# Attention values of a head as one 129-column operand, its two halves summed on VectorE

## The chip, the cores and the metric

One core of a Trainium2 chip runs the whole program. The metric is the device time of one execution in microseconds (us); lower is better. TensorE (PE) multiplies matrices, and its weight loads are listed apart (PEld). VectorE (DVE), ScalarE (ACT) and GpSimd (POOL) work element by element. SP is the queue that issues the DMAs.

## The reference

The reference is one block of a gated cross-attention transformer: `x` is (2, 256, 128), the context (2, 512, 128). The attention part is what the change touches:

```python
q1, k1, v1 = split(x1 @ Wq1), split(x1 @ Wk1), split(x1 @ Wv1)   # 8 heads of 64
k2, v2 = split(x2 @ Wk2), split(x2 @ Wv2)
k, v = concat([k1, k2]), concat([v1, v2])                        # 768 keys
attn = softmax(einsum('bihd,bjhd->bhij', q1, k) * scale)
out = einsum('bhij,bjhd->bihd', attn, v).reshape(B, N1, h * d) @ Wo + bo
x = x + tanh(g_xattn) * out
```

Behind it stands a mixture of eight experts with one shared expert (two of eight by a top-k gate, hidden width 512, exact gelu), added with a second gate.

## The kernel before, in words

Single-precision products are made from half-precision ones: a value is held as a high f16 part and a low f16 part, and high x high, high x low and low x high are summed in PSUM. There are 2 batches x 8 heads = 16 heads; two heads of a batch make a pair, and a pair has three units of 2 x 128 keys. Each engine runs its own list of instructions, written out by one loop over steps; semaphores tie the lists together. Step s handles score unit s (24 units), and other work is set beside it:

- `scores(u)` (L1105) on PE, then the exponential (`exp_unit`, L646) and the high part of the probabilities (`make_hi`, L654) on ACT, then the low part, `p_lo` = `prob` - `p_hi`, on POOL (`prob_lo`, L554; both inputs lie in SBUF).
- `max_chunk(p, c)` on PE (L1088 for c = 0 and 1, L1093 for c = 2) and `part_max` on DVE (L821) find the row maxima of the pair two or three steps ahead. Each chunk's matmul waits until DVE has finished the chunk before it, because both use the same two PSUM banks.
- `shift_row` (L1103, PE) and `shift_out` (L837, DVE) turn the maxima of a pair into the shift of its scores.
- `item_of` projects keys, queries and values of the next pairs or batch on PE (L991 to L993); ACT takes the high part out of PSUM (L635), DVE the low part (L804), one step later.
- `values(j)` (L1149) on PE multiplies the probabilities of head j with its values: 2 query tiles x 6 key tiles, three matmuls each (L1170 to L1172): `p_hi` with the 65 columns of `v_hi` (64 values and a column of ones for the sum of the row), `p_hi` with the 64 columns of `v_lo`, `p_lo` with the 65 of `v_hi`. The probabilities are the 128x128 weights. All go into one place, `o_ps`, in PSUM bank 6.
- `reciprocals(j)` (L844) and `normalise(j)` (L849) on DVE wait for `values(j)`, invert the two row sums and multiply: `o_ps` times `rsum` (in SBUF, two numbers for each row, each broadcast over 64 columns) goes to `o_sb`. `normalise` raises `o_done`, for which the next `values` waits, because there is one `o_ps`.

From step 5 on the pattern has three steps. In a step with s mod 3 = 2 (5, 8, 11, ...) PE does scores, values of a pair's first head, the shift row, the maxima c = 0, an item; with s mod 3 = 0 scores, values of the second head, the maxima c = 1, an item; with s mod 3 = 1 scores, the maxima c = 2, an item, and no values. DVE's order in a step is: low part of the item of the step before, `shift_out`, `reciprocals`, `normalise`, `part_max`. The first six pairs have their values in steps 5 to 21; maxima end with step 19. Steps 23 to 26 hold the last four heads, beside the first matmuls of the experts, which fill the rest.

```python
            def reciprocals(j):
                dve.wait_ge(pv_ps, QT * (j + 1))
                mark(nc.vector.reciprocal(rsum[:, j, :], o_ps[:, :, DH]))
```

`mark` counts an instruction, and `settle` makes DVE wait until all that are counted have been written.

Of the kernel before, what the change touches and what calls it, by code (L numbers as in the profile page):

```python
# [13 lines left out]
F32 = mybir.dt.float32  # L14
F16 = mybir.dt.float16
ALU = mybir.AluOpType
# [3 lines left out]
P = 128  # L20
B = 2
# [3 lines left out]
HEADS = 8  # L25
DH = 64
INNER = HEADS * DH
PAIRS = HEADS // 2
KEYS = T1 + T2
KT = KEYS // P  # L30
QT = T1 // P
NT = B * QT
# [21 lines left out]
KT2 = 2  # L54
UPP = KT // KT2
NPAIR = B * PAIRS
# [35 lines left out]
def chunk_of(s):  # L92

    p, c = divmod(s - CHUNK0, UPP)
    return (p, c) if 0 <= p < NPAIR else None
# [62 lines left out]
def before(n, banks):  # L158

    return max([m + 1 for m in range(n) if banks_of(m) & set(banks)], default=0)  # L160


def items_ready(*items):

    return max(ITEMS.index(it) for it in items) + 1
# [55 lines left out]
def block_kernel(nc, x, ctx_in, g_xattn, g_ffn, Wq1, Wk1, Wv1, Wk2, Wv2, Wo, bo,  # L221
                 gate_w, gate_b, w1, b1, w2, b2, ws1, bs1, ws2, bs2, out):
    stack = ExitStack()
    with stack:
        def sb(name, shape, dt):
            return stack.enter_context(nc.sbuf_tensor(name, shape, dt))

        def sem(name):
            return stack.enter_context(nc.semaphore(name))
# [9 lines left out]
        wf = sb("wf", [P, 2, NE, 2, 512], F16)  # L239
        k_both = sb("k_both", [P, B, 2, PAIRS, KEYS], F16)  # L240
        k_nat = k_both[:, :, :, :, :].rearrange("p b a h n -> p a b h n")
# [12 lines left out]
        shift = sb("shift", [P, 2, T1], F16)  # L254
        part = sb("part", [P, 2, 2, 2, QT], F32)
        nmax = sb("nmax", [P, 2, P], F32)
        v_hi = sb("v_hi", [P, B * KT, HEADS, DH + 1], F16)
        v_lo = sb("v_lo", [P, B * KT, HEADS, DH], F16)
        p_hi = sb("p_hi", [P, RINGP, 2, KT2 * T1], F16)
        p_lo = sb("p_lo", [P, RINGP, 2, KT2 * T1], F16)  # L260
        o_sb = sb("o_sb", [P, NT, INNER], F32)
# [39 lines left out]
        banks = stack.enter_context(nc.psum_tensor("banks", [P, 8, 512], F32))  # L301

        def span(first, n):

            return banks[:, first:first + 2, :].rearrange("p a n -> p (a n)")[:, 0:n]
# [7 lines left out]
            first = 2 + 2 * score_buf(u)  # L313
            return banks[:, first:first + 2, :]

        o_ps = banks[:, 6, 0:QT * (DH + 1)].rearrange("p (q d) -> p q d", q=QT)
        shift_ps_rows = banks[:, 6, 512 - P:]
        misc = banks[:, 7, :]

# [33 lines left out]
        o_done = sem("o_done")  # L353
# [29 lines left out]
        def ring_f(j):  # L383

            return ring[:, (3 + j) % RING]
# [15 lines left out]
        def item_out(n):  # L401

            kind = ITEMS[n][0]
            return span(BANK[n], KEYS) if kind == "k" else banks[:, BANK[n], :]

# [189 lines left out]
        def _(act):  # L595
# [18 lines left out]
            def item_of(n):  # L614
# [16 lines left out]
                else:  # L631
                    _, b, t = item
                    dst, s = v_hi[:, b * KT + t, :, 0:DH], 1.0 / S_W
                    src = src.rearrange("p (h d) -> p h d", d=DH)
# [97 lines left out]
        def _(dve):  # L732
# [3 lines left out]
            def mark(ins):  # L736

                nonlocal n_chain
                n_chain += 1
                ins.then_inc(dve_chain, 1)  # L740

            def settle():

                dve.wait_ge(dve_chain, n_chain)
# [35 lines left out]
            def item_of(n):  # L780
# [19 lines left out]
                else:  # L800
                    t = item[1] * KT + item[2]
                    dst, hi, s = v_lo[:, t, :, :], v_hi[:, t, :, 0:DH], 1.0 / S_W
# [39 lines left out]
            def reciprocals(j):  # L842
                dve.wait_ge(pv_ps, QT * (j + 1))
                mark(nc.vector.reciprocal(rsum[:, j, :], o_ps[:, :, DH]))  # L844

            def normalise(j):
                b, h = divmod(j, HEADS)
                settle()
                nc.vector.tensor_tensor(o_sb[:, QT * b:QT * b + QT, h * DH:(h + 1) * DH], o_ps[:, :, 0:DH],  # L849
                                        rsum[:, j, :].unsqueeze(2).broadcast_to([P, QT, DH]),  # L850
                                        ALU.mult).then_inc(o_done, 1)

# [75 lines left out]
            for i in range(CHUNK0, STEPS):  # L928
# [18 lines left out]
                if values_of(i) is not None:  # L947
                    reciprocals(values_of(i))
                    normalise(values_of(i))
                if chunk_of(i) is not None:  # L950
                    p, c = chunk_of(i)
# [9 lines left out]
                if 0 <= k < NF:  # L961
                    b, e = k // NE, EORDER[k % NE]
# [25 lines left out]
        def _(pe):  # L988
            def three(dst, w, a, start=True, stop=True):

                nc.tensor.matmul(dst, w[0], a[0], start=start, stop=False)  # L991
                nc.tensor.matmul(dst, w[0], a[1], start=False, stop=False)  # L992
                return nc.tensor.matmul(dst, w[1], a[0], start=False, stop=stop)  # L993

            def w_pair(w, cols):
                return wa[:, 0, w, cols], wa[:, 1, w, cols]

            def x_pair(cols):
                return xT[:, 0, cols], xT[:, 1, cols]
# [13 lines left out]
            def read_out(n):  # L1013

                if n > 0:
                    pe.wait_ge(item_lo, n)

            def item_of(n):
# [15 lines left out]
                elif kind == "k":  # L1034
# [6 lines left out]
                    pe.wait_ge(item_lo, ITEMS.index(("tx", 0)) + 1)  # L1041
                    last = three(dst[:, T2:KEYS], w_pair(WK1, pair), x_pair(slice(b * T1, (b + 1) * T1)))
                elif kind == "q":
# [19 lines left out]
            def q_of(p, half, hl, cols):  # L1063

                b, pp = divmod(p, PAIRS)
                return q_nat[DH * half:DH * half + DH, hl, b, pp, cols]

            def k_of(p, half, hl, cols):

                b, pp = divmod(p, PAIRS)  # L1070
                return k_nat[DH * half:DH * half + DH, hl, b, pp, cols]

            def max_chunk(p, c):
# [16 lines left out]
                else:  # L1090
                    for q in range(QT):
                        for half in range(2):
                            last = nc.tensor.matmul(banks[:, half, q * T1:(q + 1) * T1],  # L1093
                                                    q_of(p, half, 0, slice(q * P, q * P + P)),
                                                    k_of(p, half, 0, slice(T2, KEYS)), start=True, stop=True)
                last.then_inc(max_ps, 1)
# [52 lines left out]
            def values(j):  # L1149

                p, half = divmod(j, 2)
                b, h = divmod(j, HEADS)
                if j == 0:
                    read_out(before(NI, [6]))
                else:
                    pe.wait_ge(o_done, j)
                if h == 0:
                    pe.wait_ge(item_lo, items_ready(*[("v", b, t) for t in range(KT)]))
                for q in range(QT):
                    for t in range(KT):  # L1160
                        u = UPP * p + t // KT2
                        if half == 0 and q == 0 and t % KT2 == 0:
                            if u == LO_LAST:
                                pe.wait_ge(pd_done, 1)
                            else:
                                pe.wait_ge(pl_done, u + 1)
                        cols = slice(t % KT2 * T1 + q * P, t % KT2 * T1 + q * P + P)
                        vh, vl = v_hi[:, b * KT + t, h, :], v_lo[:, b * KT + t, h, :]
                        ph, pl = p_hi[:, u % RINGP, half, cols], p_lo[:, u % RINGP, half, cols]
                        nc.tensor.matmul(o_ps[:, q, :], ph, vh, start=(t == 0), stop=False, skip_group_check=True)  # L1170
                        nc.tensor.matmul(o_ps[:, q, 0:DH], ph, vl, start=False, stop=False, skip_group_check=True)  # L1171
                        last = nc.tensor.matmul(o_ps[:, q, :], pl, vh, start=False, stop=(t == KT - 1),  # L1172
                                                skip_group_check=True)
                    last.then_inc(pv_ps, 1)

# [39 lines left out]
            for i in range(CHUNK0, STEPS):  # L1215
# [3 lines left out]
                if 0 <= k < NF:  # L1219
                    b, e = k // NE, EORDER[k % NE]  # L1220
# [17 lines left out]
                    for c in range(HC):  # L1238
                        cols = slice(c * P, (c + 1) * P)
                        dst = span(2 * (k % 2), HC * T1)[:, c * T1:(c + 1) * T1]  # L1240
                        if k in H32:
                            last = nc.tensor.matmul(dst, ring_f(k)[:, 0, cols], x2T[:, tok], start=True, stop=True)  # L1242
                        else:
                            last = three(dst, (wf[:, 0, e, 0, cols], wf[:, 1, e, 0, cols]),
                                         (x2h[:, 0, tok], x2h[:, 1, tok]))
                        if c % 2 == 1:
                            last.then_inc(h_ps, 1)
                if values_of(i) is not None:
                    values(values_of(i))
# [10 lines left out]
                if 0 <= k < NF:  # L1260
# [13 lines left out]
                    for q in range(QT):  # L1274
                        for c in range(HC):
                            at = c * T1 + q * P
                            cols = slice(c * P, (c + 1) * P)
                            if k in FULL32:
                                last = nc.tensor.matmul(banks[:, 4 + k % 2, q * D:(q + 1) * D],  # L1279
                                                        hid[:, k % NHID, at:at + P], ring_f(k % NE)[:, 1, cols],  # L1280
                                                        start=(c == 0), stop=(c == HC - 1))
                                continue
                            last = three(banks[:, 4 + k % 2, q * D:(q + 1) * D],
                                         (hid_hi[:, k % HB, at:at + P], hid_lo[:, k % HB, at:at + P]),
                                         (wf[:, 0, e, 1, cols], wf[:, 1, e, 1, cols]),
                                         start=(c == 0), stop=(c == HC - 1))
# [36 lines left out]
```

## Time and profile before

| | |
|---|---|
| median of 3 runs (lowest to highest) | 157.3 us (156.89 to 157.64) |
| the profiled execution's own time | 156.95 us |
| its span, from the first to the last instruction | 155.1 us (so 1.85 us lie around it) |
| granted TensorE clock | 1.00 of full speed (2.4 GHz) in all 40 slices |
| busy: PE, PEld | 143.9 us (93%), 111.4 us (72%) |
| busy: DVE, ACT, POOL | 103.5 us (67%), 115.1 us (74%), 107.9 us (70%) |
| share of the chain that ended last | PE 73%, DVE 10%, ACT 9%, POOL 1% |

A busy engine is not yet the bound: the chain of work that ended last says what released what. The timeline lists instructions in order of time (start, duration, engine, line, operation, written tile <- read tiles, shapes, count), with the idle time before one in brackets and what ended it. Time is in us from the start of the span; where a helper is called from many places the line is the helper's. `banks` is the whole of PSUM, so an operand in PSUM is shown as `banks`; `k_both`, `prob`, `ring`, `wf`, `rsum` and `o_sb` lie in SBUF.

### The profile page before, as it was taken

To read this page: it belongs to the slowest core of one execution; us is meant where nothing else is said; L and a number is where in the kernel's file an instruction comes from. 1 tells how busy PE (TensorE), PEld (TensorE's weight loads), DVE (VectorE), ACT (ScalarE), POOL (GpSimd) and SP (SyncE) were. 2 spreads that over 40 slices of the span, in tenths; PEclk is the share of its full clock that TensorE was granted. 3 is DMA by queue.
4 is the path that set the end of the run, shared out by engine and by line. 5 is a ranking of instruction groups with operands and counts; after the bars stand their busy time and mean duration, and the time that the engine had idled before them with its cause. 6 is when DMAs were issued, how large, how long until landed. Compare 5 with 4: busy or idle time off the path is not lost.

```text
span 155.1 us, 4389 instructions
## 1 busy us (share of the span) xinstructions
PE 143.9 (93%) x1804; PEld 111.4 (72%) x1804; DVE 103.5 (67%) x215; ACT 115.1 (74%) x191; POOL 107.9 (70%) x95
## 2 busy tenths in 40 slices
PE   7789699979899999999898799999999999999992
PEld 5434354547566667657686698999999999989992
DVE  0779898888777686887763363834643779896631
ACT  3466789998988988887859988645567598968720
POOL 5506999777676667857798878965398089688730
PEclk9999999999999999999999999999999999999999
DMA  5679996000000000000000000030000000100001
GB/s 139 200 268 276 277 351 208 1 4 0 4 2 8 0 4 0 4 0 4 0 4 0 4 0 4 16 119 0 4 0 0 6 2 9 29 0 0 4 0 34
DMA packets 10253, 7.71 MB, mean 50 GB/s; under 512 B 1101, under 2 KB 8442, under 8 KB 10234
## 3 DMA queue, kind: packets, MB, share of 16 engines
q1 hardware_dynamic: 10234, 7.44, 15.8%
q8 instruction: 14, 0.23, 0.6%
q14 instruction: 5, 0.04, 0.1%
HBM read 7.18 MB, written 0.26 MB: 48 GB/s over the span
## 4 chain that ended last, share of the span: by engine, by line
PE 73%; DVE 10%; ACT 9%; issue 2%; DMA 2%; POOL 1%; SPq 0%; DVEq 0%; ACTq 0%
PE banks L1279 12%; PE banks L991 10%; PE banks L993 9%; PE banks L992 9%; PE banks L1242 5%; DVE part L821 4%; PE banks L1170 4%; ACT prob L646 3%; PE banks L1172 3%; PE banks L1171 3%; PE banks L1120 3%; PE banks L1190 2%; ACT v_hi L635 2%; DMA wf<-in_ctx_dram 2%; ACT p_hi L654 2%
## 5 line engine op out<-in xcount | busy, mean ns | idle before, releaser
L554 POOL TENSOR_TENSOR p_lo<-prob,p_hi 128x1024 f16<-128x1024 f32 x23 | 49.0, 2133 | 15.7 <-ACT p_hi L654 15.5
L710 ACT ACTIVATE prob<-banks,b1T 128x256 f32<-128x256 f32 x72 | 28.4, 475 | 12.8 <-PE banks L993 9.3
L646 ACT ACTIVATE prob<-banks 128x1024 f32<-128x1024 f32 x24 | 24.6, 1023 | 8.1 <-PE banks L1138 8.1
L821 DVE TENSOR_REDUCE part<-banks 128x2 f32<-128x1024 f32 (+1 forms) x24 | 29.0, 1216 | 1.1 <-PE banks L1093 1.0
L654 ACT ACTIVATE p_hi<-prob 128x1024 f16<-128x1024 f32 x24 | 25.4, 1057 | 0.8
L569 POOL TENSOR_TENSOR k_both<-prob,k_both 128x1024 f16<-128x1024 f32 x8 | 17.6, 2194 | 4.2 <-ACT k_both L718 3.2
L1279 PE MATMUL banks<-ring,prob 128*128 128x128 f32 x160 | 19.6, 276 | 0.0
L1170 PEld LDWEIGHTS banks<-v_hi,p_hi 128*128 128x128 f16 x192 | 17.4, 98 | 2.9 <-issue 2.5
L1170 PE MATMUL banks<-v_hi,p_hi 128*128 128x65 f16 x192 | 19.2, 195 | 0.0
L1171 PE MATMUL banks<-v_lo,p_hi 128*128 128x64 f16 x192 | 19.1, 193 | 0.0
L1172 PE MATMUL banks<-v_hi,p_lo 128*128 128x65 f16 x192 | 19.1, 194 | 0.0
L1279 PEld LDWEIGHTS banks<-ring,prob 128*128 128x128 f32 x160 | 18.8, 192 | 0.2
L1171 PEld LDWEIGHTS banks<-v_lo,p_hi 128*128 128x128 f16 x192 | 17.6, 98 | 0.2
L1172 PEld LDWEIGHTS banks<-v_hi,p_lo 128*128 128x128 f16 x192 | 17.6, 97 | 0.0
L991 PE MATMUL banks<-x2h,wf 128*128 128x256 f16 x56 | 15.3, 273 | 0.0
L992 PE MATMUL banks<-x2h,wf 128*128 128x256 f16 x56 | 15.3, 272 | 0.0
L993 PE MATMUL banks<-x2h,wf 128*128 128x256 f16 x56 | 15.3, 272 | 0.0
L934 DVE CAST k_both<-prob 128x512 f16<-128x512 f32 x8 | 10.0, 1244 | 3.2 <-ACT prob L710 3.2
L804 DVE SCALAR_TENSOR_TENSOR k_both<-banks,k_both 128x768 f16<-128x768 f32 x8 | 7.7, 956 | 5.8 <-ACT k_both L635 5.8
L991 PE MATMUL banks<-wf,k_both 128*128 128x128 f16 x64 | 11.1, 219 | 0.1
L993 PE MATMUL banks<-wf,k_both 128*128 128x128 f16 x64 | 11.1, 219 | 0.0
L992 PE MATMUL banks<-wf,k_both 128*128 128x128 f16 x64 | 11.1, 219 | 0.0
(155 smaller groups left out, 343.8 us busy)
## 6 DMA issues: line engine op xcount, KB each, us to landing
ring<-in_L_ffn_w_dram SPq DMA_DIRECT2D x16, 256.0 KB, 5.3
wf<-in_ctx_dram SPq DMA_DIRECT2D x2, 256.0 KB, 5.3
ring<-in_L_xattn_Wk_dram SPq DMA_DIRECT2D x2, 256.0 KB, 4.7
ring<-in_L_xattn_Wv_dram SPq DMA_DIRECT2D x2, 256.0 KB, 7.1
ring<-in_L_ffn_ws_dram SPq DMA_DIRECT2D x2, 256.0 KB, 6.7
x_sb<-in_x_dram SPq DMA_DIRECT2D x1, 256.0 KB, 3.0
ring<-in_L_xattn_Wq_dram SPq DMA_DIRECT2D x1, 256.0 KB, 5.0
wo<-in_L_xattn_Wo_dram SPq DMA_DIRECT2D x1, 256.0 KB, 7.8
```

What stands on the lines that cost most here:

```text
L554: nc.gpsimd.tensor_tensor(p_lo[:, u % RINGP, :, :].rearrange("p a n -> p (a n)"), prob[:, u % RINGE, :], p_hi[:, u % RINGP, :, :].rearrang ...
L646: nc.scalar.activation(prob[:, u % RINGE, :], units(u).rearrange("p a n -> p (a n)"), ACT.Exp, scale=DH ** -0.5 / S_SCORE).then_inc(exp_do ...
L654: nc.scalar.activation(p_hi[:, u % RINGP, :, :].rearrange("p a n -> p (a n)"), prob[:, u % RINGE, :], ACT.Copy).then_inc(ph_act, 1)
L710: nc.scalar.activation(hid[:, k % NHID, c * T1:(c + 1) * T1], span(2 * (k % 2), HC * T1)[:, c * T1:(c + 1) * T1], ACT.Gelu, bias=b1T[:, e ...
L821: nc.vector.tensor_reduce(dst, src, AX_X, ALU.max).then_inc(part_done, 1)
L991: nc.tensor.matmul(dst, w[0], a[0], start=start, stop=False)
L992: nc.tensor.matmul(dst, w[0], a[1], start=False, stop=False)
L993: return nc.tensor.matmul(dst, w[1], a[0], start=False, stop=stop)
L1170: nc.tensor.matmul(o_ps[:, q, :], ph, vh, start=(t == 0), stop=False, skip_group_check=True)
L1171: nc.tensor.matmul(o_ps[:, q, 0:DH], ph, vl, start=False, stop=False, skip_group_check=True)
L1172: last = nc.tensor.matmul(o_ps[:, q, :], pl, vh, start=False, stop=(t == KT - 1), skip_group_check=True)
L1279: last = nc.tensor.matmul(banks[:, 4 + k % 2, q * D:(q + 1) * D], hid[:, k % NHID, at:at + P], ring_f(k % NE)[:, 1, cols], start=(c == 0), ...
```

## The change

The values of a head are kept side by side in one buffer: 64 high values, the ones, 64 low values, 129 columns. `p_hi` is multiplied with all 129 in one matmul, so `values` issues 24 matmuls for a head, where it issued 36, and the products with the low values land in columns of their own, 65 to 128 of `o_ps`. The sum of the two halves, which PSUM made, is now made by DVE: it copies columns 0 to 63 from PSUM to the new SBUF tile `o_sum`, adds columns 65 to 128 of PSUM to it, and `normalise` reads `o_sum` in place of `o_ps`. `reciprocals(j)` also waits for `o_done` of the head before (raised by DVE itself).

```diff
+VW = 2 * DH + 1
-        v_hi = sb("v_hi", [P, B * KT, HEADS, DH + 1], F16)
-        v_lo = sb("v_lo", [P, B * KT, HEADS, DH], F16)
+        v_both = sb("v_both", [P, B * KT, HEADS, VW], F16)
+        v_hi = v_both[:, :, :, 0:DH + 1]
+        v_lo = v_both[:, :, :, DH + 1:VW]
+        o_sum = sb("o_sum", [P, QT, DH], F32)
-        o_ps = banks[:, 6, 0:QT * (DH + 1)].rearrange("p (q d) -> p q d", q=QT)
+        o_ps = banks[:, 6, 0:QT * VW].rearrange("p (q d) -> p q d", q=QT)
...
             def reciprocals(j):
                 dve.wait_ge(pv_ps, QT * (j + 1))
                 mark(nc.vector.reciprocal(rsum[:, j, :], o_ps[:, :, DH]))
+                if j > 0:
+                    dve.wait_ge(o_done, j)
+                mark(nc.vector.tensor_copy(o_sum[:, :, :], o_ps[:, :, 0:DH]))
+                settle()
+                mark(nc.vector.tensor_tensor(o_sum[:, :, :], o_sum[:, :, :], o_ps[:, :, DH + 1:VW], ALU.add))
 
             def normalise(j):
                 b, h = divmod(j, HEADS)
                 settle()
-                nc.vector.tensor_tensor(o_sb[:, QT * b:QT * b + QT, h * DH:(h + 1) * DH], o_ps[:, :, 0:DH],
+                nc.vector.tensor_tensor(o_sb[:, QT * b:QT * b + QT, h * DH:(h + 1) * DH], o_sum[:, :, :],
                                         rsum[:, j, :].unsqueeze(2).broadcast_to([P, QT, DH]),
                                         ALU.mult).then_inc(o_done, 1)
...
-                        vh, vl = v_hi[:, b * KT + t, h, :], v_lo[:, b * KT + t, h, :]
+                        vh, vboth = v_hi[:, b * KT + t, h, :], v_both[:, b * KT + t, h, :]
                         ph, pl = p_hi[:, u % RINGP, half, cols], p_lo[:, u % RINGP, half, cols]
-                        nc.tensor.matmul(o_ps[:, q, :], ph, vh, start=(t == 0), stop=False, skip_group_check=True)
-                        nc.tensor.matmul(o_ps[:, q, 0:DH], ph, vl, start=False, stop=False, skip_group_check=True)
-                        last = nc.tensor.matmul(o_ps[:, q, :], pl, vh, start=False, stop=(t == KT - 1),
+                        nc.tensor.matmul(o_ps[:, q, :], ph, vboth, start=(t == 0), stop=False, skip_group_check=True)
+                        last = nc.tensor.matmul(o_ps[:, q, 0:DH + 1], pl, vh, start=False, stop=(t == KT - 1),
                                                 skip_group_check=True)
```

## Rows read from the trace of the kernel before

**Rows 1.** Busy time by stretch: us, then PE, PEld, DVE, ACT, POOL, clock, DMA.

```profile
33.00:60.00 27.00, 26.47 (x425) 17.31 (x424) 21.29 (x37) 23.64 (x28) 19.18 (x9) 1.00 0.01 3
98.00:150.00 52.00, 51.88 (x543) 49.03 (x542) 33.72 (x74) 35.91 (x86) 35.81 (x31) 1.00 0.05 14
```

**Rows 2.** Timeline of PE, steps 9 and 10.

```profile
46.54 0.20 PE L1170 MATMUL banks<-v_hi,p_hi 128*128 128x65 f16 x1
...
47.55 0.19 PE L1170 MATMUL banks<-v_hi,p_hi 128*128 128x65 f16 x1
...
47.74 0.39 PE L1088 MATMUL banks<-k_both,qo 64*128 64x512 f16 x2
...
49.70 0.38 PE L1093 MATMUL banks<-k_both,qo 64*128 64x256 f16 x4
```

**Rows 3.** Timeline of DVE, steps 8, 9 and 11.

```profile
45.12 0.29 DVE L849 TENSOR_TENSOR o_sb<-banks,rsum 128x128 f32<-128x128 f32 x1
45.33 1.21 DVE L821 TENSOR_REDUCE part<-banks 128x2 f32<-128x1024 f32 x1
46.46 0.68 DVE L804 SCALAR_TENSOR_TENSOR v_lo<-banks,v_hi 128x512 f16<-128x512 f32 x1
47.85 0.17 DVE L844 RECIPROCAL rsum<-banks 128x2 f32<-128x2 f32 x1 [0.70 <-PE banks L1172]
48.05 0.29 DVE L849 TENSOR_TENSOR o_sb<-banks,rsum 128x128 f32<-128x128 f32 x1
48.26 1.22 DVE L821 TENSOR_REDUCE part<-banks 128x2 f32<-128x1024 f32 x1
...
54.15 0.29 DVE L849 TENSOR_TENSOR o_sb<-banks,rsum 128x128 f32<-128x128 f32 x1
```

**Rows 4.** Timeline of PE in the expert stage: f16 matmuls of 128 columns.

```profile
130.47 0.22 PE L991 MATMUL banks<-wf,k_both 128*128 128x128 f16 x1
...
131.14 0.22 PE L991 MATMUL banks<-wf,k_both 128*128 128x128 f16 x1
```

**Rows 5.** Instructions of line L849: duration ns min/median/max, first and last start.

```profile
L849 DVE TENSOR_TENSOR o_sb<-banks,rsum x16: 291/292/293, 36.5 to 97.9; 128x128 f32<-128x128 f32 x16
```

**Rows 6.** Timeline of POOL, steps 8, 9, 11, 23 and later.

```profile
45.45 2.13 POOL L554 TENSOR_TENSOR p_lo<-prob,p_hi 128x1024 f16<-128x1024 f32 x1 [0.84 <-ACT p_hi L654]
48.84 2.13 POOL L554 TENSOR_TENSOR p_lo<-prob,p_hi 128x1024 f16<-128x1024 f32 x1 [1.26 <-ACT p_hi L654]
...
54.80 2.14 POOL L554 TENSOR_TENSOR p_lo<-prob,p_hi 128x1024 f16<-128x1024 f32 x1 [0.57 <-ACT p_hi L654]
...
87.59 2.14 POOL L554 TENSOR_TENSOR p_lo<-prob,p_hi 128x1024 f16<-128x1024 f32 x1 [0.64 <-ACT p_hi L654]
90.61 1.11 POOL L585 TENSOR_TENSOR gdiff<-top 128x2 f32<-128x2 f32 x1 [0.88 <-DVE marked L898]
...
97.96 1.04 POOL L522 TENSOR_TENSOR wf<-ring,c_sw 128x512 f16<-128x512 f32 x1
...
124.28 0.20 POOL L585 TENSOR_TENSOR gdiff<-top 128x2 f32<-128x2 f32 x1 [4.45 <-DVE marked L898]
```

**Rows 7.** Timeline of DVE beside those POOL instructions.

```profile
88.88 0.29 DVE L849 TENSOR_TENSOR o_sb<-banks,rsum 128x128 f32<-128x128 f32 x1
...
90.44 1.22 DVE L917 TENSOR_TENSOR p_lo<-prob,p_hi 128x1024 f16<-128x1024 f32 x1
...
98.10 1.45 DVE L924 SCALAR_TENSOR_TENSOR wf<-ring,wf 128x512 f16<-128x512 f32 x1
```

**Rows 8.** Instructions of line L924: duration ns min/median/max, first and last start.

```profile
L924 DVE SCALAR_TENSOR_TENSOR wf<-ring,wf x11: 678/693/2040, 95.2 to 130.7; 128x512 f16<-128x512 f32 x11
```

**Rows 9.** Timeline of DVE, POOL and PE, steps 20 to 22.

```profile
82.24 0.29 DVE L849 TENSOR_TENSOR o_sb<-banks,rsum 128x128 f32<-128x128 f32 x1
...
82.51 2.13 POOL L554 TENSOR_TENSOR p_lo<-prob,p_hi 128x1024 f16<-128x1024 f32 x1
...
85.66 0.41 PE L1195 MATMUL banks<-ident,xn 128*128 128x128 f32 x2 [0.82 <-ACT xn L661]
```

## The prediction

> **What bounds the kernel now.** I read the busy time by stretch first: from 33 to 60 us, where the values are multiplied, TensorE works 26.47 of 27 us, and from 98 to 150, in the experts, 51.88 of 52 [rows 1]. So in both stages a wait put on TensorE is a loss, and what the attention loses the experts cannot give back. Next the timelines of TensorE and VectorE over one turn of the three-step pattern [rows 2, 3]. The reader is to see two things. The matmuls of a head follow each other at a steady distance. And VectorE stands close behind TensorE at one place: its second maxima (c = 1) end at 48.26 + 1.22 = 49.48, and TensorE starts the third chunk, which needs them, at 49.70, only 0.22 later.
>
> **TensorE's part.** From the first to the last L1170 of a head there are 11 sets of three in 1.01 us [rows 2]: 0.092 a set, 0.031 a matmul of 65 columns. The dropped weight load is thus hidden already, since a whole matmul with its load takes 31 ns. In the experts 12 matmuls of 128 columns take 0.67 us [rows 4], 0.056 each. A set becomes 0.056 + 0.031 = 0.087, and a head saves 12 x 0.005 = 0.06 us. The bounds for the 129-column matmul are 0.031 (a matmul costs its load, not its columns) and 0.062 (two of 65); I take 0.056, as it is measured at nearly this width. That is 0.9 us in 16 heads if nothing else moved.
>
> **VectorE's part.** Each head gains a copy from PSUM and an add with one PSUM input. The nearest row is the old normalise, which has the same 128x128 elements and a PSUM input: 0.29 us, 291 to 293 ns in all 16 [rows 5]. The bounds are a reciprocal of two elements, 0.17, and 512 elements from PSUM, 0.68 [rows 3]; I take 0.29, the row of equal size. Instructions that do not depend on each other overlap by 0.08 us (45.12 + 0.29 against 45.33), dependent ones lie 0.03 apart (47.85 + 0.17 against 48.05) [rows 3]. The copy does not depend on the reciprocal, so it starts 0.11 before the old normalise; copy, add and their two gaps take 0.64; normalise therefore starts 0.53 later after its matmuls, and with the 0.06 saved 0.47 later by the clock. The added self-wait on o_done is long fulfilled and costs nothing. The strided low values take 0, for the high values were already written at a stride. No DMA moves.
>
> **The changed inputs of normalise.** This decides. Before, its inputs were one in PSUM and one in SBUF, and it never noticed GpSimd: at 88.88 it ran its 0.29 us in the middle of a p_lo (87.59 to 89.73) [rows 6, 7]. Now o_sum and rsum both lie in SBUF. What VectorE does with two SBUF inputs beside GpSimd is in the trace. The L924 at 98.10 has two; GpSimd's L522 had started 0.14 before it, at 97.96, and ran to 99.00; L924 took 1.45 instead of 0.68 and ended at 99.55 [rows 6 to 8]. It waited for GpSimd's end and then needed 0.13 less than its full time, its start being done. It goes the other way too: L917, two SBUF inputs, ran from 90.44 to 91.66, and GpSimd's L585, started at 90.61, took 1.11 where its twin took 0.20 [rows 6, 7]. So whichever starts first makes the other wait for its end. The Trainium skill says the same on its page "SBUF — State Buffer", section "Who interferes with whom": a VectorE instruction with two SBUF inputs contends with a GpSimd instruction that reads SBUF, and the first holds the shared ports for its whole length. Our trace agrees (1.45 against 0.68). By that rule the sum is the one that follows; by the normalise rows as they stand it would be the first rival's.
>
> GpSimd's p_lo takes 2.13 us in nearly every step [rows 6], so what matters is who comes first.
>
> *First head of a pair (step 8).* Normalise would start at 45.12 + 0.47 = 45.59. p_lo starts at 45.45, after ScalarE's p_hi, which does not hang on the values. GpSimd leads by 0.14, the same lead as in the L924 row, and holds on until 47.58. Normalise ends 0.16 (0.29 - 0.13) behind it, at 47.74, not 45.41.
>
> *Who waits.* The next head's matmuls need o_done. They started at 46.54; now at 47.74 + 0.07 = 47.81 (0.07 is an estimate for the semaphore, and it stands at each handover to TensorE). From there to L1088 it took 1.20, now 1.14: 48.95. On VectorE the maxima c = 0 are queued behind normalise: 47.66 to 48.87; then the low values to 49.47, the reciprocal from 49.39, the copy from 49.48, the add, and normalise is ready at 50.12.
>
> *Second head.* GpSimd's next p_lo starts at 48.84 as before, since its scores were issued ahead of the late matmuls, and runs to 50.97. Normalise waits again and ends at 51.13. The maxima c = 1, behind it, run from 51.05 to 52.27. TensorE would be ready for the third chunk 1.96 after L1088 (47.74 to 49.70), at 50.91, but must wait to 52.34, where it started at 49.70. **The turn is 2.64 us longer.**
>
> All later scores, p_hi and p_lo move by the same 2.64, so the next pair meets the same lead. At step 11 p_lo comes a little later (54.80, normalise 54.15 + 0.47 = 54.62) [rows 3, 6], because ScalarE had a backlog there; TensorE's 1.4 us stop ahead of the third chunk gives it time to clear that, so I count the pair as well.
>
> **The sum.** Five pairs with maxima (first heads in steps 5, 8, 11, 14, 17): 5 x 2.64 = 13.2. The pair of steps 20 and 21 has none: normalise would start at 82.24 + 0.47 = 82.71, p_lo at 82.51, to 84.64 [rows 9]; it ends at 84.80 and not at 82.53, which holds the next head's matmuls by 2.3. Of this TensorE's own wait for xn, 0.82 before 85.66, and 0.06 of matmuls come back: +1.4. The last four heads stand beside the experts' matmuls, which cover VectorE's extra half microsecond; if that cover fails, an estimate is 0.5 each for three handovers, 1.5, in the range. Total 13.2 + 1.4 = 14.6, on 156.95 of the profiled execution (which is 0.35 below the median of 157.3, within its spread): **171.6 us**.
>
> **Rivals.** *1. No wait at the ports*: either a broadcast of two numbers does not count as an SBUF input, or normalise slips in ahead of p_lo. For it speaks that the lead is only 0.14; against it the L924 row with this same lead. Then only the 0.53 remains: at the third chunk 0.15 of it is slack (0.22 less the 0.07), 0.38 is waited for, 0.12 saved on two heads, +0.26 a pair, 1.3 in five, some 0.4 more in the first and last pairs: 158.7. *2. Some pairs escape*, as step 11 would by the old times: three of six at 2.64 and the rest at 0.26 is 8.7 more: 165.6. *3. Not slower: a matmul costs its load.* If 129 columns took 0.031, a head's group of 24 would take 0.73, 0.31 less than I count. At step 8 normalise would then start at 45.28, ahead of GpSimd; p_lo would wait 0.3 instead, in a queue that idles 0.84 and more before each [rows 6]. A pair saves 0.74 and pays the 0.38 at the third chunk: -0.36, some -1.5 to -2 in all, 155.3. It decides from a group shorter than 0.90 (1.04 less the lead of 0.14); the 0.056 of the 128-column rows speaks against it.
>
> **How the numbers follow.** Forecast 0.68, rival 1 0.15, rival 2 0.09, rival 3 0.08. Without rival 1 more than 2 in 10 would lie outside, so the range goes down to it, 158.2; upward it takes in the 1.5 of the last heads, the 129 columns at 0.062 and a copy somewhat over 0.29: 174.5. The forecast's own range is 169.5 to 174.5. About 0.5% is what a measurement here can tell from no change. Faster 0.05 (most of rival 3), same 0.03 (the rest), slower 0.92.
>
> **What would show it.** Normalise no longer uniform: 0.29 where GpSimd idles, up to some 2.1 us in steps with s mod 3 = 2, each ending about 0.16 behind a p_lo. Among the waits, the first matmul of the values on VectorE's o_sb, 1.3 us in some six places, and L1093's counterpart on VectorE's maxima, 1.4 in some five; before, these were small. A head's matmuls 1.04 us long in sets of 0.087. GpSimd's p_lo still 2.13, or up to 0.3 more where VectorE came first. The experts' stage unchanged in length. The prediction is wrong if normalise stays at 0.29 beside a running p_lo, or if it starts ahead of p_lo in most pairs.

## The result and the profile after

| | before | changed |
|---|---|---|
| median of 6 runs (lowest to highest) | 156.86 us (156.62 to 157.64) | 173.77 us (171.54 to 176.06) |
| ratio, with its 95% interval | 1 | 1.100 (1.092 to 1.108) |
| the profiled execution, its span | 156.95 us, 155.1 us | 173.47 us, 171.7 us |
| granted TensorE clock in the profiled execution | 1.00 | 0.99 |

The ratio leaves out the two slowest executions of the changed kernel; what sets its executions apart is in the last section.

First the page of the profile: the busy shares, the chain that ended last by engine, and two of the groups that the change touched.

```profile
span 171.7 us, 4037 instructions
...
PE 146.0 (85%) x1612; PEld 111.7 (65%) x1612; DVE 125.7 (73%) x247; ACT 115.8 (67%) x191; POOL 107.6 (63%) x95
...
PE 56%; DVE 31%; ACT 6%; issue 3%; DMA 2%; SPq 0%; DVEq 0%; ACTq 0%
...
L1178 PE MATMUL banks<-v_both,p_hi 128*128 128x129 f16 x192 | 19.1, 222 | 8.7 <-DVE o_sb L857 8.7
...
L857 DVE TENSOR_TENSOR o_sb<-o_sum,rsum 128x128 f32<-128x128 f32 x16 | 19.8, 1235 | 0.6
```

192 matmuls are gone, and TensorE is not relieved but starved: its share falls from 93% to 85%, and VectorE's part of the chain that ended last rises from 10% to 31%. VectorE's busy time rose by 22.2 us, from 103.5. The copies and adds are 8.9 of it (16 x 0.27 and 16 x 0.29), and normalise, 0.29 each time in [rows 5], now takes 1235 ns on average, which is 15.1 more. The sum, 24.0, is above 22.2 mainly because each copy overlaps the reciprocal before it by 0.08 us (47.81 + 0.16 against 47.89, below), which busy time counts once. The two new operations and normalise, in the view by tile (duration ns min/median/max):

```profile
L850 DVE COPY o_sum<-banks x16: 265/271/272, 36.6 to 114.3; 128x128 f32<-128x128 f32 x16
L852 DVE TENSOR_TENSOR o_sum<-o_sum,banks x16: 286/288/290, 36.9 to 114.6; 128x128 f32<-128x128 f32 x16
L857 DVE TENSOR_TENSOR o_sb<-o_sum,rsum x16: 291/992/2136, 37.2 to 114.9; 128x128 f32<-128x128 f32 x16
```

Copy and add have one PSUM operand and never vary. Normalise has none any more and varies by a factor of seven. The same stretch as [rows 3, 6], the timeline of VectorE in steps 8 and 9, and that of GpSimd:

```profile
47.81 0.16 DVE L847 RECIPROCAL rsum<-banks 128x2 f32<-128x2 f32 x1
47.89 0.27 DVE L850 COPY o_sum<-banks 128x128 f32<-128x128 f32 x1
48.20 0.29 DVE L852 TENSOR_TENSOR o_sum<-o_sum,banks 128x128 f32<-128x128 f32 x1
48.52 2.13 DVE L857 TENSOR_TENSOR o_sb<-o_sum,rsum 128x128 f32<-128x128 f32 x1
50.57 1.21 DVE L824 TENSOR_REDUCE part<-banks 128x2 f32<-128x1024 f32 x1
51.71 0.68 DVE L807 SCALAR_TENSOR_TENSOR v_both<-banks,v_both 128x512 f16<-128x512 f32 x1
52.31 0.15 DVE L847 RECIPROCAL rsum<-banks 128x2 f32<-128x2 f32 x1
52.38 0.27 DVE L850 COPY o_sum<-banks 128x128 f32<-128x128 f32 x1
52.68 0.29 DVE L852 TENSOR_TENSOR o_sum<-o_sum,banks 128x128 f32<-128x128 f32 x1
53.00 0.99 DVE L857 TENSOR_TENSOR o_sb<-o_sum,rsum 128x128 f32<-128x128 f32 x1
53.92 1.21 DVE L824 TENSOR_REDUCE part<-banks 128x2 f32<-128x1024 f32 x1
...
60.01 2.13 DVE L857 TENSOR_TENSOR o_sb<-o_sum,rsum 128x128 f32<-128x128 f32 x1
```

```profile
48.38 2.12 POOL L557 TENSOR_TENSOR p_lo<-prob,p_hi 128x1024 f16<-128x1024 f32 x1 [2.23 <-ACT p_hi L657]
51.72 2.12 POOL L557 TENSOR_TENSOR p_lo<-prob,p_hi 128x1024 f16<-128x1024 f32 x1 [1.22 <-ACT p_hi L657]
...
59.87 2.12 POOL L557 TENSOR_TENSOR p_lo<-prob,p_hi 128x1024 f16<-128x1024 f32 x1 [1.27 <-ACT p_hi L657]
```

The first normalise starts 0.14 behind a p_lo and ends at 50.65, 0.15 behind its end at 50.50. The second starts at 53.00 inside the next one (51.72 to 53.84) and ends 0.15 behind it too. The next pair's first p_lo starts at 59.87 and its normalise at 60.01, with the same lead. A turn is 11.49 us (48.52 to 60.01), where it was 9.03 (45.12 to 54.15) [rows 3].

Last, the timeline of TensorE in steps 9 and 10, which shows who paid, and the waits on both places over the whole run (us in total, times, longest):

```profile
50.71 0.23 PE L1178 MATMUL banks<-v_both,p_hi 128*128 128x129 f16 x1 [1.22 <-DVE o_sb L857]
...
51.87 0.39 PE L1096 MATMUL banks<-k_both,qo 64*128 64x512 f16 x2
...
55.19 0.39 PE L1101 MATMUL banks<-k_both,qo 64*128 64x256 f16 x4 [0.94 <-DVE part L824]
```

```profile
PE banks L1178 <- DVE o_sb L857: 8.7, 6, 2.3
...
PE banks L1101 <- DVE part L824: 6.9, 5, 1.9
```

The second head's matmuls wait for the first normalise (six times), the third chunk for the maxima that stand behind the second (five times). From L1096 to L1101 it takes 3.32, where it took 1.96 [rows 2]. Together that is 15.6 us of idle TensorE, of which 1.1 stood before a third chunk already in the kernel before:

```profile
PE banks L1093 <- DVE part L821: 1.1, 2, 0.5
```

### The profile page after: what moved, and what is told of

It reads as the page before. It is cut to its first block, busy times and chain, and to the rows that moved or that the text cites. A ratio compares the mean times of both kernels' runs of the same rounds, so it can differ in the third digit from the quotient of the medians.

```text
span 171.7 us, 4037 instructions
## 1 busy us (share of the span) xinstructions
PE 146.0 (85%) x1612; PEld 111.7 (65%) x1612; DVE 125.7 (73%) x247; ACT 115.8 (67%) x191; POOL 107.6 (63%) x95
## 4 chain that ended last, share of the span: by engine, by line
PE 56%; DVE 31%; ACT 6%; issue 3%; DMA 2%; SPq 0%; DVEq 0%; ACTq 0%
PE banks L1286 10%; DVE o_sb L857 10%; DVE part L824 9%; PE banks L999 8%; PE banks L1001 7%; PE banks L1000 7%; PE banks L1249 4%; PE banks L1178 4%; PE banks L1197 3%; ACT prob L649 2%; DMA wf<-in_ctx_dram 2%; DVE o_sum L852 2%; PE banks L1179 2%; DVE v_both L807 2%; DVE shift L840 2%
## 5 line engine op out<-in xcount | busy, mean ns | idle before, releaser
L649 ACT ACTIVATE prob<-banks 128x1024 f32<-128x1024 f32 x24 | 24.6, 1024 | 16.3 <-PE banks L1146 15.6
L1178 PE MATMUL banks<-v_both,p_hi 128*128 128x129 f16 x192 | 19.1, 222 | 8.7 <-DVE o_sb L857 8.7
L1178 PEld LDWEIGHTS banks<-v_both,p_hi 128*128 128x128 f16 x192 | 16.8, 97 | 11.9 <-DVE o_sb L857 10.4
L857 DVE TENSOR_TENSOR o_sb<-o_sum,rsum 128x128 f32<-128x128 f32 x16 | 19.8, 1235 | 0.6
L1179 PE MATMUL banks<-v_both,p_lo 128*128 128x65 f16 x192 | 18.5, 193 | 0.0
L1179 PEld LDWEIGHTS banks<-v_both,p_lo 128*128 128x128 f16 x192 | 17.0, 98 | 0.2
L638 ACT ACTIVATE v_both<-banks 128x512 f16<-128x512 f32 x12 | 6.9, 598 | 5.5 <-PE banks L1001 5.5
```

Source lines behind the costliest of these rows:

```text
L649: nc.scalar.activation(prob[:, u % RINGE, :], units(u).rearrange("p a n -> p (a n)"), ACT.Exp, scale=DH ** -0.5 / S_SCORE).then_inc(exp_do ...
L1178: nc.tensor.matmul(o_ps[:, q, :], ph, vboth, start=(t == 0), stop=False, skip_group_check=True)
L1179: last = nc.tensor.matmul(o_ps[:, q, 0:DH + 1], pl, vh, start=False, stop=(t == KT - 1), skip_group_check=True)
```

## The experiments

Each run is given beside runs of the kernel before on the same chip. My theory was that the ports cost some 13 us, the longer VectorE chain some 2, and that the matmuls give back less than one. The rivals: the chain itself, GpSimd's load, or a two-input normalise that always loses.

### Take away the second SBUF input alone

```diff
-        rsum = sb("rsum", [P, NH, QT], F32)
...
+        rsum = banks[:, 6, 300:300 + NH * QT].rearrange("p (j q) -> p j q", q=QT)
```

> The changed kernel, with one edit: the inverted row sums lie in PSUM, so normalise has the same three VectorE instructions of the same shapes before and in it, but one SBUF input (o_sum) and not two. Theory (normalise waits for GpSimd at the shared SBUF ports): all 16 normalises take about 0.29 us, TensorE's waits on VectorE's o_sb vanish, and the time falls to about 158.7, which is what the added copy and add alone are worth. Rival A (the longer chain of VectorE instructions itself is the cost): the time stays at 171 to 174 and normalise still takes up to 2.1 us.

Measured 158.57 us (4 runs, 158.48 to 158.83) beside 156.93; ratio 1.012 (1.010 to 1.014). Normalise in this kernel, duration ns min/median/max:

```profile
L857 DVE TENSOR_TENSOR o_sb<-o_sum,banks x16: 286/286/289, 37.1 to 100.0; 128x128 f32<-128x128 f32 x16
```

Number, order and shapes of the instructions are those of the changed kernel; two numbers per row and head have moved from SBUF to PSUM. TensorE's waits for `o_sb` fall from 8.7 us in six places to 0.5 in one, and 13 us of the loss are gone (171.50, the fastest execution of the changed kernel, at a mean clock of 1.00, less 158.57). Rival A falls.

### Two SBUF inputs, but in time

```diff
                 mark(nc.vector.reciprocal(rsum[:, j, :], o_ps[:, :, DH]))
+                if j > 0:
+                    dve.wait_ge(o_done, j)
+                mark(nc.vector.tensor_copy(o_sum[:, :, :], o_ps[:, :, 0:DH]))
...
-                nc.vector.tensor_tensor(o_sb[:, QT * b:QT * b + QT, h * DH:(h + 1) * DH], o_ps[:, :, 0:DH],
+                nc.vector.tensor_tensor(o_sb[:, QT * b:QT * b + QT, h * DH:(h + 1) * DH], o_sum[:, :, :],
```

> The kernel before, 36 matmuls a head, with only a copy of o_ps to an SBUF tile added, from which normalise reads: so normalise has two SBUF inputs, but starts only about 0.19 us later than before (45.31 in step 8, with p_lo at 45.45). Theory (whichever engine starts first makes the other wait): VectorE now leads by 0.14, normalise stays at 0.29 in the first heads of the pairs, the p_lo behind it takes up to 0.3 more, and the time is 157 to 158.5. Rival B (a normalise with two SBUF inputs loses to GpSimd whatever the order, or runs slowly beside it): several normalises of 1 to 2 us and a time of 165 or more.

Measured 157.41 us (10 runs) beside 156.93; ratio 1.004 (1.002 to 1.006). The first head of step 8, VectorE and GpSimd in this kernel:

```profile
45.78 0.29 DVE L853 TENSOR_TENSOR o_sb<-o_sum,rsum 128x128 f32<-128x128 f32 x1
...
45.92 2.14 POOL L555 TENSOR_TENSOR p_lo<-prob,p_hi 128x1024 f16<-128x1024 f32 x1 [1.03 <-ACT p_hi L655]
```

The lead of 0.14 is now VectorE's, and the same two-input normalise costs 0.29. So the second SBUF input is not dear in itself: it is dear when it comes second. Rival B falls. A miss in a detail: p_lo was not 0.3 longer but took 2.14, up to 2.21 once. Normalise ended 0.15 after p_lo's start here, and that overlap cost p_lo 0.01; the next experiment has an overlap of 0.27 that costs it 0.14. So I estimate from these two that some 0.13 at the start of a p_lo can pass beside normalise. Four of the last five heads, which start inside some GpSimd instruction, took 0.39 to 0.81, where TensorE hardly waits for them (0.2 us in one place).

### Make GpSimd later, by giving it more work

```diff
                 pool.wait_ge(ph_act, u + 1)
+                link(nc.gpsimd.memset(pause[:, :], 0.0))
+                link(nc.gpsimd.memset(pause[:, :], 0.0))
```

> The changed kernel, with two one-column memsets on GpSimd between the wait for p_hi and each p_lo, so that every p_lo starts some 0.3 us later (GpSimd has more work). Theory (order decides): the lead of 0.14 that p_lo has in the first heads turns into a lag, normalise takes 0.29 there, and the time falls to about 159 to 161. Rival C (GpSimd's load or the number of its instructions is what slows VectorE): the same as the changed kernel or slower, 172 to 176.

> The changed kernel with one one-column memset on GpSimd ahead of each p_lo: by the run with two, which moved p_lo by 0.34 us, this moves it by about 0.17, so that p_lo and normalise of a first head start within 0.05 us of each other, VectorE ahead by a little. Theory (the first one wins, with no band between): VectorE wins, about 158.6. Rival E (the ports are taken some time ahead of the recorded start on GpSimd, so that it wins at equal starts): near the changed kernel's 171 to 174.

With two memsets ahead of each p_lo 158.70 us (4 runs, 158.43 to 158.87) beside 156.93: 46 added GpSimd instructions make the changed kernel 13 us faster (from 171.50), and rival C falls. With one memset 161.52 (160.35 to 162.07) beside 156.79, between the two cases, so I looked at who started first. Normalise in the first heads of steps 8, 17 and 20 of this kernel, and the p_lo beside it:

```profile
46.46 0.29 DVE L859 TENSOR_TENSOR o_sb<-o_sum,rsum 128x128 f32<-128x128 f32 x1
...
74.83 0.29 DVE L859 TENSOR_TENSOR o_sb<-o_sum,rsum 128x128 f32<-128x128 f32 x1
...
84.81 2.24 DVE L859 TENSOR_TENSOR o_sb<-o_sum,rsum 128x128 f32<-128x128 f32 x1
```

```profile
46.48 2.27 POOL L559 TENSOR_TENSOR p_lo<-prob,p_hi 128x1024 f16<-128x1024 f32 x1
...
74.84 2.27 POOL L559 TENSOR_TENSOR p_lo<-prob,p_hi 128x1024 f16<-128x1024 f32 x1
...
84.78 2.12 POOL L559 TENSOR_TENSOR p_lo<-prob,p_hi 128x1024 f16<-128x1024 f32 x1
```

VectorE ahead by 0.01 or 0.02: 0.29, and p_lo pays 0.14. GpSimd ahead by 0.03: 2.24. If there is a band between, or an advantage for one engine, it is narrower than these few hundredths, against rival E. The one lost race in this trace, in step 20, cost TensorE 2.45 us of waiting, and that is the most of what this run is above 158.7 (the rest of it is in the last section). The Trainium skill, "SBUF — State Buffer", section "Who interferes with whom", has the sentence "Issue order, not op shape, decides who blocks"; these runs agree, down to 0.03 us.

### The two parts of the change alone

The kernel before with a copy and an add of the same shapes ahead of normalise, which still reads PSUM:

```diff
+                mark(nc.vector.tensor_copy(o_sum[:, :, :], o_ps[:, :, 0:DH]))
+                settle()
+                mark(nc.vector.tensor_tensor(o_sum[:, :, :], o_sum[:, :, :], o_ps[:, :, 0:DH], ALU.add))
```

> VectorE's part alone: the kernel before, 36 matmuls a head, normalise from PSUM as before, with a copy and an add of the same shapes put ahead of normalise (their sum is written and not used). Theory (0.53 us later per head, of which 0.38 is waited for at the third chunk): 1.7 to 2.3 above the kernel before, 158.7 to 159.3, a little above the changed kernel with its row sums in PSUM (158.57), which has the shorter matmul group as well. Rival F (the copy and add are hidden): 157.

Measured 158.95 us (4 runs, 158.74 to 159.21) beside 156.79: +2.2, ratio 1.013 (1.010 to 1.016). So the copy and the add are not hidden (rival F). And the changed kernel's matmuls with normalise straight from PSUM:

```diff
-                mark(nc.vector.tensor_copy(o_sum[:, :, :], o_ps[:, :, 0:DH]))
-                settle()
-                mark(nc.vector.tensor_tensor(o_sum[:, :, :], o_sum[:, :, :], o_ps[:, :, DH + 1:VW], ALU.add))
...
-                nc.vector.tensor_tensor(o_sb[:, QT * b:QT * b + QT, h * DH:(h + 1) * DH], o_sum[:, :, :],
+                nc.vector.tensor_tensor(o_sb[:, QT * b:QT * b + QT, h * DH:(h + 1) * DH], o_ps[:, :, 0:DH],
```

> TensorE's part alone: 24 matmuls a head, 12 of them of 129 columns, and normalise reads columns 0 to 63 from PSUM as before; no copy and no add, so the products of the high probabilities with the low values are left out of the result. Theory (a matmul costs its columns, 0.056 us for 129): 0.06 us saved a head, 156.0 to 156.6 where the kernel before has 156.9. Rival D (a matmul costs its weight load, 0.031 us): 0.37 saved a head where TensorE is the bound, 151.5 to 153.5.

Measured 156.54 us (12 runs) beside 156.93: -0.4, ratio 0.998 (0.997 to 0.999). Two L1172 of one head in this kernel, eleven sets apart on TensorE's timeline:

```profile
46.69 0.23 PE L1172 MATMUL banks<-v_both,p_hi 128*128 128x129 f16 x1
...
47.66 0.22 PE L1172 MATMUL banks<-v_both,p_hi 128*128 128x129 f16 x1
```

That is 0.97 / 11 = 0.088 a set where it was 0.092: with 12 weight loads fewer and as many columns as before (129 + 65 against 65 + 64 + 65), a head is 0.04 us shorter, so a matmul costs its columns here and not its load. Rival D falls. The parts add up: +2.2 - 0.4 = 1.8, against the 1.6 of the first experiment, where both stand together without the ports.

### A version that repairs it

If the ports are out of the way, the third chunk still waits for the maxima behind the longer chain. Nobody needs the second head's normalise soon, so the maxima can go first:

```diff
+                maxima_first = chunk_of(i) is not None and chunk_of(i)[1] == 1
+                if maxima_first:
+                    part_max(*chunk_of(i))
                 if values_of(i) is not None:
                     reciprocals(values_of(i))
                     normalise(values_of(i))
...
-                    part_max(p, c)
+                    if not maxima_first:
+                        part_max(p, c)
```

With the row sums in PSUM as well:

> The changed kernel with its row sums in PSUM, and in the steps of a pair's second head VectorE takes the maxima c = 1 ahead of the reciprocal, copy, add and normalise, which nobody needs before the step after next. Theory (what was left of the loss is the wait of the third chunk for the maxima c = 1 behind the longer chain): the waits of 0.5 to 1.0 before the third chunk vanish, 156.0 to 156.8, no slower than the kernel before. Rival H (the longer chain moves the wait elsewhere, to the next head's matmuls or the low parts of the items): 158 or more.

And on the kernel before:

> The kernel before with the same reordering alone: 36 matmuls, one VectorE instruction fewer in the chain. Theory: the two waits of 0.53 before a third chunk (steps 7 and 19) vanish, about 155.8 to 156.4; if the reordered changed kernel is not below this, the 129 columns are worth nothing even with the ports and the wait out of the way.

The first took 157.07 us (12 runs), the second 156.89 (12 runs), the kernel before beside them 156.84; ratios 1.0015 (1.0002 to 1.0029) and 1.0005 (0.9989 to 1.0021). The reordering takes 1.5 us off the repaired change, so the third chunk was what it still waited for, but it stops short of the 156.0 to 156.8 expected. TensorE's waits show why, with the row sums in PSUM alone and then with the maxima first as well:

```profile
PE banks L1101 <- DVE part L824: 2.6, 5, 1.0
PE banks L999 <- DVE v_both L807: 1.1, 2, 0.9
```

```profile
PE banks L1003 <- DVE v_both L807: 1.7, 2, 0.9
...
PE banks L1105 <- DVE part L824: 0.9, 2, 0.5
```

The third chunk gains 1.7, and 0.6 comes back at an item that waits for the low part of the values: rival H's mechanism, at a smaller price than it named. No version that computes the whole result beats the kernel before, and since the reordered change is not below the reordered kernel before, the 129 columns with their copy and add bring nothing here, even with the ports and that wait out of the way. On the kernel before, the expected 0.5 to 1 us did not come: in step 7 the wait falls only from 0.53 to 0.45, for the chunk c = 1 leaves TensorE some 0.3 us behind the values, and the old reciprocal and normalise filled just that gap.

### Is the rest TensorE's clock?

The changed kernel's executions spread over 4.5 us, those of the kernel before over 1.0. In these two kernels TensorE does products of the unit matrix before it waits for normalise or the maxima, into PSUM banks that are free then (`n` is 8 and then 4, twice that in step 21):

```diff
+            def fill(s, n):
...
+                for _ in range(n):
+                    nc.tensor.matmul(banks[:, bank, 0:120], ident[:, :], ident[:, 0:120], start=True, stop=True)
```

> The changed kernel; where TensorE waits for normalise or for the maxima (steps 6 to 21), it first does 8 (step 21: 16) products of the unit matrix with itself, some 0.9 us, into PSUM banks that nobody uses then. Theory (the part of the loss above 14.6, and the spread from 171.5 to 176, come from TensorE's clock, granted at half after its long idle stretches): clock 1.00 in all runs, all within 171 to 173, although TensorE has more to do. Rival G (the spread has nothing to do with TensorE's idle time): the same mean clocks of 0.97 to 1.00 and a spread of 171.5 to 176, or slower.

> The changed kernel once more, beside the next one on the same chip. Theory (its spread is TensorE's clock after long idle stretches): again a spread of 3 us or more, from about 171.5 where the clock is granted in full to 174 to 176 where it is not.

> The kernel with the busy TensorE, with half as many extra products, because 8 took 2.0 us in the trace and outlasted the waits of 1.3 to 1.4: now 4 (step 21: 8), about 1.0 us, which fits into each wait. Theory (clock): clock 1.00, all executions within about 1 us of each other, at 171.0 to 172.5, the lower end of the changed kernel. Rival G (the spread is not the clock's): as wide a spread as the changed kernel, or a median above it.

The first overshot: its 8 products took 2.0 us on TensorE's timeline and outlasted the waits. It took 176.23 us, outside the 171 to 173 expected, but its five executions lay within 0.9 (175.97 to 176.88), all at a mean clock of 1.00. The changed kernel again: 174.47 (6 runs, 171.50 to 176.10). With 4 products, on the same chip: 171.93 (171.59 to 173.43), five of six within 0.6 us and at 1.00. So with useless work in TensorE's waits the changed kernel is 2.5 us faster in the median. With filling 10 of 11 executions had a mean clock of 1.00, without it 3 of 12, so rival G falls. The one at 173.43 had a mean clock of 0.99: in these few runs the filling made the loss rare, not impossible.

## Why the prediction was right

171.6 was forecast, 173.77 measured; of the changed kernel's 12 executions the three at a mean clock of 1.00 took 171.50 to 171.79.

**TensorE's part: the size was off.** I took 0.056 for 129 columns and 0.06 saved a head; a set takes 0.088 and a head saves 0.04. In the sum that is nothing; it is why the repaired versions gain so little.

**VectorE's part: right.** Copy and add were taken at 0.29 and measured 0.27 and 0.29. Rival 1, which is this part without the ports, was priced at 158.7; with the ports taken out the kernel runs in 158.57. The 0.07 for a handover to TensorE stood without a row; it measured 0.06 (normalise's end at 50.65, the matmuls at 50.71).

**The changed inputs: right, and the heart of it.** The L924 and L585 rows [rows 6 to 8] had shown the contention on other instructions, and it held for normalise though one of its inputs is only two numbers, broadcast. The lead that decided was forecast at 0.14 and was 0.14, in step 8 and again in step 11; that it came back in every pair made one lost race six. To the hundredth this is luck: from the reciprocal's start to normalise's it takes 0.51 more and not 0.53 (0.71 against 0.20 [rows 3]), and the matmuls save 0.04 and not 0.06, so two errors cancel. Step 11, which would have escaped by the old times, did not, as argued: ScalarE's exponential, which had followed the work ahead of it without a wait, now waits 0.17 for TensorE there, so the backlog is gone. No pair escaped, against rival 2. Rival 3 was priced with a GpSimd queue that idles 0.84 and more before each p_lo; [rows 6] show 0.57 and 0.64 as well, which still has room for its 0.3.

**Who waits, and the sum: right.** In steps 8 and 9 normalise took 2.13 (2.15 by my times) and 0.99 (1.01), and that turn is 2.46 longer (2.64). Over all five turns the forecast of 13.2 is met. From the first normalise of step 5 to that of step 20 the kernel before takes 45.72 us (to 82.24 [rows 9]), and the changed kernel, in its execution of 171.50 us, 58.88, which is 13.16 more:

```profile
36.52 0.29 DVE L849 TENSOR_TENSOR o_sb<-banks,rsum 128x128 f32<-128x128 f32 x1
```

```profile
36.83 2.13 DVE L857 TENSOR_TENSOR o_sb<-o_sum,rsum 128x128 f32<-128x128 f32 x1
...
95.71 2.07 DVE L857 TENSOR_TENSOR o_sb<-o_sum,rsum 128x128 f32<-128x128 f32 x1
```

From there to the end of the span it loses another 1.1 (forecast 1.4), and 0.3 lies ahead of step 5. In the profiled execution of 173.47 us normalise of step 20 began at 97.68, inside a p_lo that had begun at 97.48, and took 2.07. The experts' stage gave nothing back: from 112 to 164 us TensorE was busy 52.00 of 52.

```profile
112.00:164.00 52.00, 52.00 (x535) 49.07 (x534) 35.82 (x80) 36.73 (x91) 37.28 (x33) 1.00 0.05 14
```

**What was missing.** The 2 us between 171.6 and 173.8 have a cause that the prediction did not name: what TensorE's new idle time can do to its clock. The range held the median only by the room that it left for other terms (the last heads, the 129 columns, the copy), which is luck, and two of the six executions lie above its 174.5.

## What to carry to other kernels

Before an operand is moved from PSUM to SBUF, count the SBUF inputs of every instruction that reads it, and look at what GpSimd runs at that moment: a small instruction on VectorE can become as long as GpSimd's (here 0.29 became 2.13 beside a p_lo of 2.12), and all that is queued behind it waits too. Where such a pair can't be avoided, who starts first decides, so a few tenths of a microsecond of order, or one tiny operand left in PSUM, are worth more than the work that was saved. And matmuls that already follow each other at the pace of their columns gain almost nothing from fewer weight loads (here 0.4 us of 157).

## What the runs showed of the hardware that was not expected

The profiled execution of the changed kernel (173.47 us), busy time in short stretches (us, then PE, PEld, DVE, ACT, POOL, granted clock, DMA):

```profile
88.00:90.00 2.00, 0.41 (x8) 0.11 (x4) 1.97 (x3) 1.52 (x2) 0.96 (x1) 1.00 0.00 0
90.00:92.00 2.00, 1.70 (x13) 1.49 (x14) 1.47 (x3) 0.56 (x1) 1.36 (x1) 0.81 0.00 0
92.00:94.00 2.00, 2.00 (x11) 1.73 (x12) 0.23 (x2) 0.00 (x0) 0.76 (x1) 0.50 0.00 0
94.00:96.00 2.00, 2.00 (x35) 1.57 (x32) 1.15 (x5) 0.70 (x1) 0.60 (x2) 0.84 0.03 8
```

TensorE worked 0.41 of 2 us, waiting for the maxima behind a normalise, and soon after its clock was granted at half, 1.2 GHz and not 2.4, for some 3 us. What fell into it was the output projection, L1197:

```profile
90.30 0.39 PE L1101 MATMUL banks<-k_both,qo 64*128 64x256 f16 x4 [1.90 <-DVE part L824]
90.63 3.27 PE L1197 MATMUL banks<-wo,k_both 128*128 128x128 f32 x16
```

The same place in the execution of 171.50 us, where the clock stayed at 1.00:

```profile
89.93 0.39 PE L1101 MATMUL banks<-k_both,qo 64*128 64x256 f16 x4 [1.89 <-DVE part L824]
90.25 2.05 PE L1197 MATMUL banks<-wo,k_both 128*128 128x128 f32 x16
```

The same 16 matmuls take 3.27 us and 2.05. So a wait can be paid twice: once as idle time, and once in the work behind it. Over the 12 executions of the changed kernel time and mean clock go together: 171.5 to 171.8 at 1.00, 173.3 to 173.5 at 0.99, 174.1 to 175.0 at 0.98, 175.7 to 176.1 at 0.97. The kernel with one memset shows it too: behind the one lost race in step 20 the clock was 0.50 from 88 to 90 us, and its one execution with a mean clock of 1.00 took 160.35, the other three 161.32 to 162.07. Not every such wait brings it: in the execution of 173.47 us a wait of 1.90 ahead of 43.69 us and one of 2.29 ahead of 99.81 left the clock at 1.00, and in that of 171.50 none of the waits lowered it. Nor is the kernel before safe: one of 23 executions of it beside the first experiments took 235.53 us at a mean clock of 0.56, and no trace shows why. Why some waits and executions escape was not tried and stays open.
